# Perceiver layer, cross-attention: order of VectorE's and TensorE's turns, query chunks at the start, and which queue issues the early loads

## What is computed

```
x: [32, 64, 256]   ctx_1024: [32, 1601, 256]
q = _layernorm(x) @ Wq + bq ; k = ctx @ Wk + bk ; v = ctx @ Wv + bv     # all [.., 256]
attn = einsum('bqd,bkd->bqk', q, k)                                     # one head, 1601 keys
result = softmax(attn) @ v
y = result + _layernorm(x)
x = x + ((y - mean(y)) * rsqrt(var(y) + 1e-5) * gamma + beta)
```

## Time and profile before

| | us |
|---|---|
| median of 3 runs | 659.53 (653.05 to 661.37) |
| the profiled execution | 654.53, its span on the core 652.8 |
| TensorE busy | 522.8 (80%) |
| VectorE busy | 399.7 (61%) |
| ScalarE busy | 188.1 (29%) |
| GpSimd busy | 197.9 (30%) |
| mean granted clock of TensorE | 0.919 of 2.4 GHz |
| moved by DMA | 109.79 MB |

### The profile page before, as it was taken

How to read it: one execution, slowest core, us unless ns; L and a number is a source line. 1 busy time by engine, 2 the same in 40 slices (tenths; PEclk the granted TensorE clock), 3 DMA queues, 4 the chain that set the end, 5 groups by cost and what they waited for, 6 DMA issues and landing times.

```text
span 652.8 us, 14254 instructions
## 1 busy us (share of the span) xinstructions
PE 522.8 (80%) x4842; PEld 358.1 (55%) x4843; DVE 399.7 (61%) x1031; ACT 188.1 (29%) x565; POOL 197.9 (30%) x298
## 2 busy tenths in 40 slices
PE   5556988979897979898956899998899438999920
PEld 4323555646565656555635677776445236888810
DVE  3726659787978888787532578787553023343427
ACT  2214112222222222231302344343320014555510
POOL 4100201111111112011211465656227712555530
PEclk9969798989898989899987999999999859999975
DMA  8965274766666665752314865440003223444338
GB/s 298 387 232 149 76 255 163 251 240 238 251 235 249 239 248 208 268 194 91 91 34 148 246 182 184 147 137 0 2 17 106 105 65 95 130 134 139 109 118 269
DMA packets 65034, 109.79 MB, mean 168 GB/s; under 512 B 6964, under 2 KB 46054, under 8 KB 65001
## 3 DMA queue, kind: packets, MB, share of 16 engines
q1 hardware_dynamic: 56828, 96.46, 43.5%
q0 software_dynamic: 3792, 8.42, 3.7%
q10 hardware_dynamic: 4380, 4.47, 2.3%
HBM read 86.34 MB, written 24.94 MB: 170 GB/s over the span
## 4 chain that ended last, share of the span: by engine, by line
PE 54%; DMA 16%; DVE 14%; issue 4%; ACT 3%; another core or an unknown queue 3%; ACTq 3%; POOL 2%; SPq 1%; DVEq 0%; POOLq 0%
DMA ring<-in_ctx_dram 9%; PE bank L906 8%; PE bank L926 8%; PE bank L1220 6%; DVE ctxT L1306 5%; PE bank L1140 4%; PE bank L1005 3%; PE bank L1232 3%; PE bank L1175 3%; PE bank L916 2%; DVE blockmax L1318 2%; PE bank L1044 2%; DMA rbias_b<-n_L_ffn_router_bias_dram 2%; PE bank L1214 2%
## 5 line engine op out<-in xcount | busy, mean ns | idle before, releaser
L1306 DVE STREAM_TRANSPOSE ctxT<-ring 128x832 f32<-128x832 f32 x128 | 122.6, 1013 | 45.8 <-DMA ring<-in_ctx_dram 23.7
L906 PE MATMUL bank<-ctxT,qT_all 32*64 32x416 f32 (+2 forms) x2048 | 99.5, 526 | 8.9 <-DMA rbias_b<-n_L_ffn_router_bias_dram 5.6
L926 PE MATMUL bank<-ring,prob 128*64 128x256 f32 (+1 forms) x832 | 93.4, 381 | 0.0
L730 ACT ACTIVATE prob<-bank,negmax 128x416 f32<-128x416 f32 (+2 forms) x80 | 41.0, 528 | 169.9 <-DVE negmax L1328 169.9
L906 PEld LDWEIGHTS bank<-ctxT,qT_all 32*64 32x64 f32 x2048 | 59.1, 140 | 42.1 <-issue 20.1
L926 PEld LDWEIGHTS bank<-ring,prob 128*64 128x64 f32 (+1 forms) x832 | 58.3, 137 | 33.4 <-issue 5.6
L563 POOL TENSOR_TENSOR var<-mv,eps 128x1 f32<-128x1 f32 x32 | 6.1, 190 | 227.8 <-DVE mv L1351 190.5
L652 POOL DMA_INDIRECT expert_out<-prob,dest x47 | 46.2, 984 | 56.2 <-DVE prob L1638 32.1
L916 PE MATMUL bank<-ident,prob 128*128 128x128 f32 (+1 forms) x208 | 33.7, 326 | 23.5 <-ACT prob L730 23.5
L1220 PE MATMUL bank<-ring,ctxT 128*128 x188 | 49.0, 383 | 0.6 <-ACT ctxT L814 0.4
L916 PEld LDWEIGHTS bank<-ident,prob 128*128 128x128 f32 (+1 forms) x208 | 28.9, 168 | 30.4 <-ACT prob L730 29.1
(11 more groups left out here) (211 smaller groups left out, 880.5 us busy)
## 6 DMA issues: line engine op xcount, KB each, us to landing
ring<-in_ctx_dram SPq DMA_DIRECT2D x48, 1024.0 KB
qT_all<-q_by_pair SPq DMA_DIRECT2D x13, 512.0 KB
ctxT<-rows_by_expert SPq DMA_DIRECT2D x47, 128.5 KB
rows_by_expert<-blank SPq DMA_DIRECT2D x12, 385.5 KB, 3.5
mid<-stage SPq DMA_DIRECT2D x32, 128.0 KB
ring<-in_ctx_dram SPq DMA_DIRECT2D x16, 130.0 KB
x_all<-in_x_dram SPq DMA_DIRECT2D x4, 512.0 KB, 10.2
ctxT<-mid SPq DMA_DIRECT2D x16, 128.0 KB, 2.4
```

Of the source, the lines that this page charges most:

```text
L730: act.activation(to, of, ACT.Exp, bias=negmax[:, 0:1], accum_out=sums[:, n:n + 1]).then_inc(exp_done, 1)
L906: last = pe.matmul(S[a][64 * b:64 * b + 64, 0:KW[a]], q_rep[mine, r, c, 64 * b:64 * b + 64], ctxT[mine, c, b, 0:KW[a]], start=c == 0, stop ...
L926: last = pe.matmul(U[64 * b:64 * b + 64, 0:D], probT[0:rows, k, 64 * b:64 * b + 64], ring[0:rows, r, b, k, :], start=k == 0, stop=k == KT)
L1306: dve.transpose(ctxT[:, c].rearrange("p b (k j) -> p (b k) j", j=Q), ring[:, r].rearrange("p b k c -> p (b k) c")[:, :, columns(c):columns ...
```

## The change

In the loop: VectorE's turn takes the maxima before any block turn of the next pair (EARLY falls away), and residual(i-2) moves from ahead of normalise(i-1) to directly ahead of first_norm(i-2). TensorE's turn i flips pair i-2 instead of i-1, right behind scores(i), and project(i-2) moves behind weigh(i-1).

At the start: only chunks 0 and 1 come before scores(0); chunk 2 follows it, chunk 3 follows scores(1). The key bias (`key_bias`, and ScalarE's copy `bk_row`) moves ahead of chunk 1. SyncE issues all of the chunks' stores, the first three query loads and the late loads: chunk 0's stores behind the x loads, a wait for them, the query load of pair 0, context 1, chunk 1's stores, query loads 1 and 2, context 2, the late loads, and the stores of chunks 2 and 3. VectorE takes the statistics of x parts 2 and 3 ahead of both normalisations. The wait for the late loads on TensorE moves from ahead of scores(1) to ahead of turn 2.

```diff
     KW = [KT * Q + max(0, min(Q, TAIL - Q * a)) for a in range(QUADS)]
     EXPS = [(a, lo, hi) for a in range(QUADS) for lo, hi in ((0, KW[a] // Q * Q), (KW[a] // Q * Q, KW[a])) if lo < hi]
     KG = 4
-    EARLY = 5
     KPARTS = [range(lo, min(lo + KG, KT + 1)) for lo in range(0, KT + 1, KG)]
     LN_EPS = 1e-5
     RING = 3
...
                                  stage[64 * b:64 * b + 64, :, :].rearrange("p a c -> p (a c)")).then_inc(stored, 16)
             sp.sem_inc(stored, 32)
+            def store_q(n):
+                m = STAGED[n]
+                sp.wait_ge(qT_copied, 2 * n + 2)
+                to = q_dram[4 * n:4 * n + 4].rearrange("i j (a x) -> j i a x", a=QUADS)
+                for a in range(QUADS):
+                    sp.dma_start(to[:, :, a, :], q_stage[m][Q * a:Q * a + Q].rearrange("j i d s -> j i (d s)"))\
+                        .then_inc(q_stored[m], 16)
             load_x(0)
             load_x(1)
             sp.wait_ge(tails_ready, RING)
             load(0, 0)
             load_x(2)
             load_x(3)
+            store_q(0)
+            sp.wait_ge(q_stored[0], 16 * QUADS)
+            load_q(0, 0)
             load(1, 1)
+            store_q(1)
+            load_q(1, 1)
+            load_q(2, 2)
             sp.wait_ge(wT_done, 2)
             load(2, 2)
+            sp.dma_start(wv[:, :, :], t["L0_xattn_Wv"].rearrange("(k p) f -> p k f", p=P)).then_inc(rest_loaded, 16)
+            for to, of in ((bv_b, "L0_xattn_bv"), (gamma_b, "L0_xattn_gamma"), (beta_b, "L0_xattn_beta")):
+                sp.dma_start(to[:, :], t[of].partition_broadcast(P)).then_inc(rest_loaded, 16)
+            sp.dma_start(bq2_col[:, :], t["L0_attn_b_q"].rearrange("(p a) -> p a", a=1)).then_inc(rest_loaded, 16)
+            sp.dma_start(bout_b[:, :], t["L0_attn_b_out"].partition_broadcast(P)).then_inc(rest_loaded, 16)
+            sp.dma_start(rbias_b[:, :], t["L0_ffn_router_bias"].partition_broadcast(P)).then_inc(rest_loaded, 16)
+            store_q(2)
+            store_q(3)
             def follow(i, r, stores=True):
...
                     act.wait_ge(qT_done, 2 * n + dc + 1)
                     act.activation(q_stage[m][:, :, dc, :], bank[6 + dc][:, :].rearrange("p (i s) -> p i s", i=4),
                                    ACT.Identity, bias=bqk_col[:, dc:dc + 1]).then_inc(qT_copied, 1)
-                act.wait_ge(qT_copied, 2 * n + 2)
-                to = q_dram[4 * n:4 * n + 4].rearrange("i j (a x) -> j i a x", a=QUADS)
-                for a in range(QUADS):
-                    act.dma_start(to[:, :, a, :], q_stage[m][Q * a:Q * a + Q].rearrange("j i d s -> j i (d s)"))\
-                        .then_inc(q_stored[m], 16)
             rows_turned(0)
             act.wait_ge(wqk_done, 2)
             act.copy(bqk_col[:, :], bank[3][:, 300:300 + DH]).then_inc(wqk_copied, 1)
             act.wait_ge(wqk_copied, 2)
             query_blocks(0)
+            act.wait_ge(wqk_done, 3)
+            act.copy(bk_row[:, :], bank[3][:, 0:D + 1]).then_inc(bk_row_copied, 1)
             rows_turned(1)
             query_blocks(1)
-            act.wait_ge(q_stored[0], 16 * QUADS)
-            for r in range(RING):
-                act.dma_start(q_rep[:, r, :, :].rearrange("p c s -> p (c s)"), q_of(r)).then_inc(q_loaded[r], 16)
-            act.wait_ge(wqk_done, 3)
-            act.copy(bk_row[:, :], bank[3][:, 0:D + 1]).then_inc(bk_row_copied, 1)
-            rows_turned(2)
-            query_blocks(2)
-            act.dma_start(wv[:, :, :], t["L0_xattn_Wv"].rearrange("(k p) f -> p k f", p=P)).then_inc(rest_loaded, 16)
-            for to, of in ((bv_b, "L0_xattn_bv"), (gamma_b, "L0_xattn_gamma"), (beta_b, "L0_xattn_beta")):
-                act.dma_start(to[:, :], t[of].partition_broadcast(P)).then_inc(rest_loaded, 16)
-            act.dma_start(bq2_col[:, :], t["L0_attn_b_q"].rearrange("(p a) -> p a", a=1)).then_inc(rest_loaded, 16)
-            act.dma_start(bout_b[:, :], t["L0_attn_b_out"].partition_broadcast(P)).then_inc(rest_loaded, 16)
-            act.dma_start(rbias_b[:, :], t["L0_ffn_router_bias"].partition_broadcast(P)).then_inc(rest_loaded, 16)
             def turned_out(i):
...
                 if ahead:
                     exps(i)
+            rows_turned(2)
+            act.wait_ge(q_stored[1], 16 * QUADS)
+            exps(0)
+            query_blocks(2)
+            turned_out(0)
             rows_turned(3)
-            act.wait_ge(q_stored[1], 16 * QUADS)
-            turn(0, back1=False, back2=False)
+            exps(1)
             query_blocks(3)
-            turn(1, back2=False)
             with act.Fori(2, PAIRS) as i:
                 turn(i)
             turn(PAIRS, ahead=False)
...
             last.then_inc(wqk_done, 1)
             pe.wait_ge(wqk_copied, 2)
             queries_of(0)
+            key_bias()
             queries_turned(1)
             queries_of(1)
-            key_bias()
-            queries_turned(2)
-            queries_of(2)
             def scores(i, r, round_):
...
-            def turn(i, r, round_, ahead=True, back1=True, back2=True):
+            def turn(i, r, round_, ahead=True, back1=True, back2=True, back3=True):
                 if ahead:
-                    if back1:
-                        pe.wait_ge(probT_copied, (i - 1) * len(KPARTS) + 2)
+                    pe.wait_ge(probT_copied, (i - 1) * len(KPARTS) + 2)
                     scores(i, r, round_)
                 if back2:
+                    if back3:
+                        pe.wait_ge(res_ready, i - 2)
+                    flip(i - 2)
+                if back1:
+                    pe.wait_ge(Un_ready, i - 1)
+                    weigh(i - 1, (r - 1) % RING)
+                if back2:
                     project(i - 2)
-                if back1:
-                    if back2:
-                        pe.wait_ge(Un_ready, i - 1)
-                    else:
-                        pe.wait_ge(qT_copied, 4 * DH)
-                    weigh(i - 1, (r - 1) % RING)
                 if ahead:
                     turn_probs(i)
-                if back1:
-                    if back2:
-                        pe.wait_ge(res_ready, i - 1)
-                    flip(i - 1)
             pe.wait_ge(bk_row_copied, 1)
             scores(0, 0, 0)
+            queries_turned(2)
+            queries_of(2)
+            pe.wait_ge(xnT_copied, 3 * DH)
+            turn_probs(0)
+            pe.wait_ge(probT_copied, 2)
+            scores(1, 1, 0)
+            pe.wait_ge(probT_copied, 4)
             queries_turned(3)
             queries_of(3)
+            pe.wait_ge(qT_copied, 4 * DH)
+            weigh(0, 0)
             pe.wait_ge(xnT_copied, 4 * DH)
-            turn_probs(0)
+            turn_probs(1)
             pe.wait_ge(rest_loaded, 112)
-            turn(1, 1, 0, back2=False)
-            turn(2, 2, 0)
+            turn(2, 2, 0, back3=False)
             with pe.Fori(0, (PAIRS - RING) // RING) as it:
                 for u in range(RING):
                     turn(it * RING + (RING + u), u, it + 1)
...
                 if back3:
                     second_norm(i - 3)
-                if more:
-                    blocks_turned(i + 1, (r + 1) % RING, round_ + (1 if r == RING - 1 else 0), range(0, EARLY))
                 if ahead:
                     block_max(i)
                     row_max(i)
                 if more:
-                    blocks_turned(i + 1, (r + 1) % RING, round_ + (1 if r == RING - 1 else 0), range(EARLY, BLOCKS))
-                if back2:
-                    residual(i - 2)
+                    blocks_turned(i + 1, (r + 1) % RING, round_ + (1 if r == RING - 1 else 0), range(BLOCKS))
                 if also:
                     dots(*also)
                 if back1:
...
                 if ahead:
                     row_sum(i)
                 if back2:
+                    residual(i - 2)
                     first_norm(i - 2)
             for c in range(BLOCKS):
                 block_turned(0, 0, c, 0)
             x_statistics(2)
+            x_statistics(3)
             x_normed(2)
-            x_statistics(3)
             x_normed(3)
             dve.wait_ge(bk_row_copied, 1)
             dots(0, 4)
```

## The result

| | before | changed |
|---|---|---|
| median, us | 658.66 (653.05 to 661.37, 4 runs) | 677.31 (669.02 to 681.3, 4 runs) |
| the profiled execution, us | 654.53, span 652.8 | 681.3, span 679.6 |
| B(3), us | 111.50 | 117.40 |
| B(15), us | 317.48 | 343.4 |
| mean turn between them, us | 17.17 | 18.84 |

The changed kernel takes 1.0265 of the time of before, 95% interval 1.0197 to 1.0334: slower, since the whole interval lies above 1; 632 us were forecast. All ratios here compare the faster runs of each kernel, those within 1.5% of its fastest one. Between the two profiled executions lie 26.8 us of span: 5.9 at the start (up to B(3)), 20.0 in the twelve turns, 0.9 behind them.

What follows compares the result with a forecast made beforehand. Neither VectorE nor TensorE was full; every second 17.17 us turn waited for a context load, maxima standing behind block turns. Start -10.9, loop -14.5, end +0.6 gave -24.8 from 654.53: 629.7, stated as 632 us, range 624 to 641 (chance 0.60).

Steps and rivals of the forecast that it cites:

- The turn of VectorE: Loop: 15.41 us of work plus 0.55 waiting for GpSimd's deviation, 15.96 a turn; twelve turns save 14.5 us.
- The load is 7 us early: Loop: the context load lands at B(i)+11, its block turns start at B(i)+18.5 (B(i): start of pair i's maxima).
- I add nothing: Loop: four DMA engines carry 15.9 us a turn; backlog may grow 0.2 against 5 to 7 of slack, uncharged.
- Rival (e): Loop: four DMA engines saturate, making the kernel slower; decides above 18.1 us a turn, 671 us at 19.5; chance 0.05.
- the argument against it: Loop: the 99.3% DMA share with a context load is already the full rate, and it is reached now.
- The start: Up to pair 3's maxima: scores(0) at 30.9, weigh(0) at 65.4, those maxima at 100.6, 10.9 us earlier.
- its wait for ScalarE's copy of chunk 3: Start, TensorE: weigh(0) waits for the copy, which waits for chunk 2's stores; a new wait of 6 us.
- The end: From pair 15's maxima to the last second norm: 27.6 us against 27.03, +0.6.
- TensorE: Loop: 2.9 us ahead of VectorE each turn, idling about 1.2 us a turn, so VectorE stays the bound.

Runs made afterwards that it cites:

- a1: The changed order of VectorE's and TensorE's turns in the loop, with the start of the kernel before; 639.8 us, ratio 0.985 to before.
- a3: The changed kernel with every query load cut into four loads of 32 partitions; 614.6 us, ratio 0.948 to before.
- b3: The changed kernel with only the loop's query loads (pairs 3 to 15) cut into four loads of 32 partitions; 633.2 us, ratio 0.978 to before.
- f2: The changed kernel with the two stage stores per pair cut into eight of 16 partitions; 640.0 us, ratio 0.986 to before.
- b1: a3 with VectorE issuing residual(i-2) ahead of normalise(i-1) and row_sum(i), first_norm(i-2) behind them; 605.5 us, ratio 0.935 to before.
- b2: The changed kernel with SyncE waiting for query load 0 before it issues context load 1; 663.6 us, ratio 1.017 to before.
- b4: The changed kernel with only the first three query loads cut into four loads of 32 partitions; 653.7 us, mean turn 18.61 us.

## Why the forecast was wrong, step by step

**The turn of VectorE: right.** 15.96 us were forecast from 15.41 of work and 0.55 for GpSimd. Where the loads are early (a1's first turns, a3, b3, f2) it is 16.2 to 16.3; the wait measured 0.70 and not 0.55, the rest is a little more work. That the new wait can be taken out again b1 shows: 15.5, the 15.41 of the work.

**"The load is 7 us early", "I add nothing": the step that failed.** The four engines were seen, their work a turn was counted, 15.9 us against a turn of 15.96, and nothing was charged. The count took each transfer at its time when it runs alone, and the slack of 5 to 7 us was to absorb the rest. It did not: VectorE waited for the context load in 11 of 12 turns, the turn was 18.84 us and not 15.96, which is 34.6 of the 51.6 us between forecast and measurement (the two profiled executions). Cutting the loop's query loads alone (b3) brings the turn to 16.26, spreading the stores alone (f2) as well. By the Trainium skill (DMA: Bandwidth & Descriptors, "Why a DMA increments its semaphore by 16 and not by 1") the outermost sizes set the number of engines. The traces agree: shares of 12.9% with 2 and 26.0% with 4.

**The price of a late load was missing.** The forecast counted one loop through the load, over the maxima. The other, from the landing over the second norm and the store to the parts queued behind it on SyncE, exists in the kernel before too; there the four engines had 17.17 us for 15.9, and the chain did not run over it. Rival (e) named the four engines and a deciding point of 18.1 us a turn; it came to 18.84. (By its own terms, -10.9 and +0.6, the point is 18.0, and a turn of 19.5 gives 672.) Its chance of 0.05 was too small, because the argument against it took the 99.3% of a context load as proof that nothing slows. In that row the query load was issued at 168.79, behind the whole context load; the trace of before has none in which it stands just ahead of one. Even (e) had half of the mechanism: it charged the engines' work, and the runs show a closed way over SyncE beside it.

**The start: wrong by 16.8 us.** B(3) was forecast at 100.6 and came at 117.40. Query load 0 beside context load 1 was taken at 5.15 us behind its issue and took to about 38: scores(0) are 7.7 late, and b2 wins 6.1 of them back. All that follows on SyncE was placed by landing times, with issuing free; SyncE was held 11.39 us in chunk 1's stores, then 8.54 in Wv's load. (The 9.82 at 68.93 are not such a hold: they include the wait for ScalarE's copy of chunk 3, which itself waits until 75.69 for chunk 2's stores.) So weigh(0) came at 77.00, 11.6 late, and its wait for ScalarE's copy of chunk 3 (5.98, forecast 6) is the right wait at the wrong time. The last 6.3 us came between scores(2) and B(3): VectorE waited 6.43 us for context load 3 at 102.17. That the start is sound with all query loads cut a3 shows: B(3) at 91.7, better than forecast.

**The end:** +0.6 forecast, +0.9 measured.

**TensorE:** as forecast it bounds nothing where the loads are early. Its clock granted in the loop is 0.99 in a3 against 0.95 before, and 0.92 in the changed kernel, where it idles more.

## To carry over

Sum the work of a turn for each DMA engine, not for the queue, and at the times that transfers take beside each other; when the fullest engine has as much work as the new turn is long, a shorter turn of VectorE buys little (a1), and an order on the issuing queue that makes late transfers later can turn it into a loss. Look for the cheap cure first: the same query bytes cut into loads of outermost size 32 took 8% off here (ratio 0.948 against 1.027). Then try the change's parts again on that better base; two edits that were worth nothing and a loss alone gave 5% together, and one more edit (b1) made it 6.5%.

## Of the hardware, not expected

- A query load on 4 engines just ahead of a context load on 16: both together 174 to 207 GB/s with a DMA share of 1.02 to 1.05, at 28 to 36 and at 84 to 92 us (353 and 339 with that load cut, b3); the context load alone 419, the query load alone mostly 98 to 106. In the loop, where the query load is issued 11 us ahead of the parts (239.99 and 250.79), it was 338 and 321 GB/s at 254 to 258 and 258 to 262 us. Why is not known.
- SyncE is held in issuing when loads of few engines are outstanding: four stores 11.39 us (1.82 otherwise), the load of 256 KB for Wv 8.54 us, and 8.17 in b3, where in b1 and b4, with the first three query loads cut, it was 0.95 and 0.38.
- The start is not free of this with cut query loads either: a3 moves 238 GB/s from 40 to 44 us at a share of 1.03. Query loads, context load 2 and the late loads overlap there; which of them slows was not separated.
